# ScalarE's order of work in two edge convolutions, and node ranks from a product with a step matrix instead of 49 gathers

## The reference, cut to what matters

```python
def mesh_conv(x, src, dst, ea, w1, b1, g, bt, w2, b2):
    m = jnp.concatenate([x[dst], x[src], ea], axis=-1) @ w1 + b1
    m = jax.nn.silu(group_norm(m, g, bt))          # 8 groups of 16
    m = m @ w2 + b2
    out = jax.ops.segment_sum(m, dst, num_segments=n)
    cnt = jax.ops.segment_sum(jnp.ones((dst.shape[0],), m.dtype), dst, num_segments=n)
    return out / jnp.clip(cnt, 1.0)[:, None]
h = mesh_conv(x, ...); h = silu(group_norm(h)) + time embedding
h = mesh_conv(h, ...); h = silu(group_norm(h)) + x          # then attention, then GAT
```

## Time and profile before

| | us |
|---|---|
| median of three runs | 11735.4 |
| the runs | 11731.89 to 11742.31 |
| profiled execution, its own time | 11847.93 |
| its span in the trace | 11846.2 |
| `prepare` and `n_first`, span's start to the first gather of convolution 1 | 238.64 |
| convolution 1, first gather to the last copy of sums | 238.64 to some 2730 |
| last copy of sums of convolution 2 | 5343.66 |

### The profile page before, as it was taken

The page is one execution under the profiler, slowest core; times in us unless marked ns, Lnnn a source line. Parts: engine busy times, 40 slices in busy tenths (PEclk is TensorE's granted clock), DMA queues, the critical chain, the costliest instruction groups (busy, mean ns, idle before and its releaser), DMA issues. The chain is left out here.

```text
span 11846.2 us, 181243 instructions
## 1 busy us (share of the span) xinstructions
PE 8134.7 (69%) x44314; PEld 6471.6 (55%) x44314; DVE 6838.3 (58%) x16254; ACT 4174.9 (35%) x19386; POOL 6469.9 (55%) x6618
## 2 busy tenths in 40 slices
PE   2677777775777777774666666666467777777775
PEld 1455455553555555553555555555367667777774
DVE  4677777775777777775545555555633333333336
ACT  0344444442444444441222222222123333333332
POOL 4666666662666666642555555554155555555551
PEclk7888888887888888886777777777578788888886
DMA  4344344442434444433554444554344444444443
GB/s 109 107 113 114 112 112 114 113 114 60 113 112 114 113 113 113 113 97 107 144 146 144 143 143 143 144 144 115 84 94 96 96 95 98 97 96 98 99 97 89
DMA packets 1667963, 1323.24 MB, mean 112 GB/s; under 512 B 578730, under 2 KB 1444339, under 8 KB 1666782
## 3 DMA queue, kind: packets, MB, share of 16 engines
q1 hardware_dynamic: 1427212, 770.46, 23.7%
q0 software_dynamic: 237088, 539.87, 17.6%
q10 hardware_dynamic: 2610, 1.32, 0.1%
HBM read 1250.67 MB, written 60.09 MB: 111 GB/s over the span
## 5 line engine op out<-in xcount | busy, mean ns | idle before, releaser
L537 POOL DMA_INDIRECT conv_gath<-b,plan x3232 | 3060.8, 947 | 2007.9 <-issue 866.6
L890 POOL DMA_INDIRECT gat_gath<-g,idx x1616 | 1756.4, 1087 | 1540.6 <-DVE gat_val L1171 861.2
L890 POOL DMA_INDIRECT attn_gath<-kv,plan x1616 | 1528.5, 946 | 1429.6 <-DVE attn_val L1171 746.3
L573 PE MATMUL conv_sums<-conv_hot,conv_m 128*128 128x128 f32 x6464 | 1271.8, 359 | 1261.0 <-ACT acc L610 553.5
L573 PEld LDWEIGHTS conv_sums<-conv_hot,conv_m 128*128 128x128 f32 x6464 | 1100.2, 257 | 1670.5 <-issue 1670.4
L593 ACT ACTIVATE conv_sq<-conv_z 128x512 f32<-128x512 f32 x808 | 482.2, 597 | 2276.7 <-PE conv_z L563 1917.9
L925 PE MATMUL gat_p_edge<-weta,plan 128*128 128x136 f32 x3232 | 862.8, 355 | 522.0 <-ACT gat_edge L1000 255.8
L656 DVE TENSOR_REDUCE conv_var<-conv_sq 128x32 f32<-128x512 f32 x808 | 549.4, 680 | 1153.2 <-ACT conv_sq L593 960.5
L560 PEld LDWEIGHTS conv_z<-conv_win,conv_hotT 128*128 128x128 f32 x6464 | 923.1, 205 | 514.0 <-issue 514.0
L1025 ACT COPY small<-attn_smalls 40x127 f32 x1616 | 417.3, 258 | 1987.8 <-remote 1490.4
L556 PE MATMUL conv_z<-conv_wblock,conv_ea 128*128 128x512 f32 x1616 | 988.1, 698 | 82.6 <-DVE conv_hotT L647 37.9
(11 more groups left out here) (370 smaller groups left out, 15956.4 us busy)
## 6 DMA issues: line engine op xcount, KB each, us to landing
conv_win<-a SPq DMA_DIRECT2D x3232, 64.0 KB
conv_places<-places SPq DMA_DIRECT2D x202, 512.0 KB
attn_win<-q SPq DMA_DIRECT2D x1616, 64.0 KB
plan<-in_xeT SPq DMA_DIRECT2D x404, 256.0 KB
conv_gath<-b,plan POOLq DMA_INDIRECT x3232
attn_places<-places SPq DMA_DIRECT2D x101, 512.0 KB
plan<-places SPq DMA_DIRECT2D x404, 128.0 KB
attn_gath<-kv,plan POOLq DMA_INDIRECT x1616
```

Source lines behind the costliest of these rows:

```text
L537: pool.indirect_dma_start(gath[:, b.c * BQ + k, t, :], None, b_table, bass.IndirectOffsetOnAxis(ap=C["src"][:, b.quad(k) * QT + t:b.quad(k ...
L573: mm = nc.tensor.matmul(sums[g % SQ][:, t * P:(t + 1) * P], m[:, g % BQ, t * P:(t + 1) * P], hot[:, g % BQ, t, :], start=True, stop=True)
L890: pool.indirect_dma_start(gath[:, b.c * BQ + k, t, :], None, table, bass.IndirectOffsetOnAxis(ap=rows, axis=0))\
```

## The change

In `conv_edges`, ACT's order becomes, for each p: square of 2p+4, copies of quads 2p-2 and 2p-1, SiLU of 2p, square of 2p+5, SiLU of 2p+1, with one turn of the loop fewer. No instruction is added or taken away there, and PE's, DVE's and POOL's orders stay.

The tile in which a node falls is now found in `prepare` without gathers. Two small DMAs bring the 1616 first-node numbers as 101 rows of 16, and the same rows moved by one. POOL writes the node numbers 0 to 6271 in 101 partitions. DVE forms the differences of the rows (`steps`, 101x17) and a 101x6272 matrix that is 1 where a batch begins below a node (`reached`). 49 matmuls of 101x128 by 101x17 add up the steps, which gives for each node the 16 first-node numbers of its batch and the number of the batch. DVE finds the tile from that (ten operations). The destinations' 49 gathers stay in `n_first` and no longer wait for anything there; part 0 of the count stands behind group 4 instead of 5.

```diff
 # prepare, SyncE
             sp.wait_ge(padded, 1)
+            by_batch = w["n0_b"].rearrange("o (k t) -> (o k) t", t=TB)
+            sp.dma_start(starts_k[:, 0, :], by_batch).then_inc(starts_loaded, 16)
+            sp.dma_start(starts_k[1:NBATCH, 1, :], by_batch[0:NBATCH - 1, :]).then_inc(starts_loaded, 16)
+            sp.wait_ge(padded, 2)
             for dst, src in edge_loads:
 # prepare, GpSimd
             pool.iota(node_i[:, :], pattern=[[P, NBLK]], base=0, channel_multiplier=1).then_inc(pool_made, 1)
+            pool.iota(nodes_i[:, :], pattern=[[1, NP]], base=0, channel_multiplier=0).then_inc(nodes_made, 1)
 # prepare, TensorE
+            pe.wait_ge(reached_made, 1)
+            for part, (b0, b1) in enumerate(RANKED):
+                for b in range(b0, b1):
+                    mm = nc.tensor.matmul(p_n[part][:, (b - b0) * (TB + 1):(b - b0 + 1) * (TB + 1)],
+                                          reached[:, b * P:(b + 1) * P], steps[:, :], start=True, stop=True)
+                mm.then_inc(starts_ready, 1)
             pe.wait_ge(loaded, LOADS)
 # prepare, VectorE
+            nc.vector.memset(starts_k[0:1, 1, :], 0).then_inc(padded, 1)
             nc.vector.memset(dst_q[:, :], N).then_inc(padded, 1)
...
+            dve.wait_ge(starts_loaded, 2 * 16)
+            link(nc.vector.tensor_copy(first_k[:, :], starts_k[:, 0, 0:1]))
+            link(nc.vector.memset(first_k[0:1, :], -1.0))
+            link(nc.vector.tensor_tensor(steps[:, 0:TB], starts_k[:, 0, :], starts_k[:, 1, :], ALU.subtract))
+            link(nc.vector.memset(steps[:, TB:TB + 1], 1.0))
+            dve.wait_ge(nodes_made, 1)
+            link(nc.vector.tensor_scalar(reached[:, :], nodes_i[:, :], first_k[:, 0:1], None, ALU.is_gt))
+            dve.sem_inc(reached_made, 1)
             dve.wait_ge(edges_loaded, EDGE_LOADS)
-            link(nc.vector.tensor_copy(n0_f[:, :], n0_all[:, :].rearrange("p (k t) -> p k t", t=TB)[:, :, 0]))
-            link(nc.vector.tensor_tensor(below[:, :, 0:NBATCH], bc(n0_f[:, :].unsqueeze(1), wide),
-                                         bc(node[:, :].unsqueeze(2), wide), ALU.is_lt))
-            link(nc.vector.tensor_reduce(batch[:, :], below[:, :, 0:NBATCH], AX.X, ALU.add))
-            link(nc.vector.tensor_scalar(batch[:, :], batch[:, :], -1.0, 0.0, ALU.add, ALU.max))
-            link(nc.vector.tensor_copy(batch_i[:, :], batch[:, :]))
...
             dve.sem_inc(places_made, 1)
+            for part, (b0, b1) in enumerate(RANKED):
+                dve.wait_ge(starts_ready, part + 1)
+                link(nc.vector.tensor_tensor(below[:, bs, 0:TB], pn[:, :, 0:TB], bc(node[:, bs].unsqueeze(2), wide), ALU.is_lt))
+                link(nc.vector.tensor_reduce(tile[:, 0, bs], below[:, bs, 0:TB], AX.X, ALU.add))
+                # ... and three more small operations to tile_i
 # conv_edges, ScalarE
-            for p in range(-2, NPAIR + 2):
-                g = 2 * p - 4
+            for p in range(-2, NPAIR + 1):
+                g = 2 * p - 2
...
+                square(2 * p + 4)
                 copies(g, starts)
                 copies(g + 1, starts)
                 silu(2 * p)
-                square(2 * p + 4)
+                square(2 * p + 5)
                 silu(2 * p + 1)
-                square(2 * p + 5)
 # n_first, GpSimd
                 for part, (b0, b1) in enumerate(RANKED):
-                    for b in range(b0, b1):
-                        pool.indirect_dma_start(n0_rows[:, b, :], ...)
-                for part, (b0, b1) in enumerate(RANKED):
-                    pool.wait_ge(tile_found, part + 1)
                     for b in range(b0, b1):
                         pool.indirect_dma_start(dst_rows[:, b, :], ...)
 # n_first, VectorE
-                    if g == 1:
-                        find_tiles(dve, link, 0)
-                    if g == 3:
-                        find_tiles(dve, link, 1)
-                    if g == 5:
+                    if g == 4:
                         rank(dve, link, 0)
```

More of the change, by code:

```diff
@@ L203, in prepare @@
         node_i = st.sb("node_i", [P, NBLK], I32)
-        n0_f = st.sb("n0_f", [P, NBATCH])
-        node, below, batch, batch_i = (R[n] for n in ("node", "below", "batch", "batch_i"))
+        starts_k = st.sb("starts_k", [NBATCH, 2, TB], I32)
+        first_k = st.sb("first_k", [NBATCH, 1])
+        steps = st.sb("steps", [NBATCH, TB + 1])
+        nodes_i = st.sb("nodes_i", [NBATCH, NP], I32)
+        reached = st.sb("reached", [NBATCH, NP])
+        node, below, tile_i = (R[n] for n in ("node", "below", "tile_i"))
         tile, shift, corner = (R[n] for n in ("tile", "shift", "corner"))
@@ L226, in prepare @@
         p_rep = st.ps("p_rep", [P, 512])
+        p_n = [st.ps(f"p_n{n}", [P, 512]) for n in range(2)]
+        starts_loaded, nodes_made, reached_made, starts_ready = (
+            st.sem(n) for n in ("starts_loaded", "nodes_made", "reached_made", "starts_ready"))
         edges_loaded, loaded, stored = st.sem("edges_loaded"), st.sem("loaded"), st.sem("stored")
@@ L366, in _ @@
             link = Chain(dve, chain)
-            wide = [P, NBLK, NBATCH]
+            nc.vector.memset(starts_k[0:1, 1, :], 0).then_inc(padded, 1)
             nc.vector.memset(dst_q[:, :], N).then_inc(padded, 1)
@@ L395, in _ @@
             dve.sem_inc(places_made, 1)
+            for part, (b0, b1) in enumerate(RANKED):
+                bs, wide = slice(b0, b1), [P, b1 - b0, TB]
+                dve.wait_ge(starts_ready, part + 1)
+                pn = p_n[part][:, 0:(b1 - b0) * (TB + 1)].rearrange("p (b t) -> p b t", t=TB + 1)
+                link(nc.vector.tensor_tensor(below[:, bs, 0:TB], pn[:, :, 0:TB], bc(node[:, bs].unsqueeze(2), wide), ALU.is_lt))
+                link(nc.vector.tensor_reduce(tile[:, 0, bs], below[:, bs, 0:TB], AX.X, ALU.add))
+                link(nc.vector.scalar_tensor_tensor(tile[:, 0, bs], pn[:, :, TB], float(TB), tile[:, 0, bs], ALU.mult, ALU.add))
+                link(nc.vector.tensor_scalar(tile[:, 0, bs], tile[:, 0, bs], -1.0 - TB, 0.0, ALU.add, ALU.max))
+                link(nc.vector.tensor_copy(tile_i[:, bs], tile[:, 0, bs]))
             link(nc.vector.memset(mask[:, :, :], -BIG))
@@ L1377, in node_stage @@
         if kind == "first":
-            n0_gathered, dst_gathered = ([st.sem(f"{n}{h}") for h in range(2)] for n in ("n0_gathered", "dst_gathered"))
-            tile_found, ranked, degree_ready, rank_chain = (
-                st.sem(n) for n in ("tile_found", "ranked", "degree_ready", "rank_chain"))
+            dst_gathered = [st.sem(f"dst_gathered{h}") for h in range(2)]
+            ranked, degree_ready, rank_chain = (st.sem(n) for n in ("ranked", "degree_ready", "rank_chain"))
         LOADS = 16 * {"first": 1, "conv1": 0, "conv2": 1, "attn": 3, "gat": 3}[kind]
@@ L1748, in node_stage @@
         if kind == "first":
[L1749 to L1762, removed]
+            node, below, tile = (R[n] for n in ("node", "below", "tile"))
+            dst_rows, tile_i, degree = (R[n] for n in ("dst_rows", "tile_i", "degree"))
             def rank(dve, link, part):
@@ L1783, in _ @@
                 for part, (b0, b1) in enumerate(RANKED):
-                    for b in range(b0, b1):
-                        pool.indirect_dma_start(n0_rows[:, b, :], None, w["n0_b"].rearrange("o (k t) -> (o k) t", t=TB),
-                                                bass.IndirectOffsetOnAxis(ap=batch_i[:, b:b + 1], axis=0))\
-                            .then_inc(n0_gathered[part], 16)
-                for part, (b0, b1) in enumerate(RANKED):
-                    pool.wait_ge(tile_found, part + 1)
                     for b in range(b0, b1):
@@ L1858, in build @@
             R = {"node": kept("node", [P, NBLK]), "below": kept("below", [P, NBLK, P]),
-                 "n0_rows": kept("n0_rows", [P, NBLK, TB], I32), "dst_rows": kept("dst_rows", [P, NBLK, P], I32),
-                 "batch": kept("batch", [P, NBLK]), "batch_i": kept("batch_i", [P, NBLK], I32),
+                 "dst_rows": kept("dst_rows", [P, NBLK, P], I32),
                  "tile": kept("tile", [P, 2, NBLK + 1]), "tile_i": kept("tile_i", [P, NBLK], I32),
```

## The result

The changed kernel takes 11,641.3 us (median of 4 runs, 11,636.3 to 11,657.3) against 11,738.0 us before (median of 4). The ratio is 0.992, with a 95% interval of 0.9903 to 0.9938, so the gain is some 97 us, or 0.8%. The forecast was 11,670 us, a gain of 64, in a range of 11,560 to 11,790. Sign and range held. The two terms of the sum were off in opposite directions, and one step of the reasoning behind them was wrong: about half of the gain came from a part that the sum had at 8 us.

What follows compares the result with a forecast made beforehand. POOL's gathers were taken to bound the steady convolutions. `prepare` -7.4, `n_first` -48.4, tails -8 and steady pairs 0 made -64 us, so 11735.4 became 11,670 us, in a range of 11,560 to 11,790.

Steps and rivals of the forecast that it cites:

- The gathers set the steady cycle: Steady convolutions: a gather costs 1.4 to 1.5 us, and eight of them are the cycle of a pair.
- The low rival: Convolutions: ACT's order holds the cycle, which would fall to 10.0 us a pair, 10,910 us in all; chance 0.06.
- So I take zero for the steady pair: Steady convolutions: the new ACT order gains nothing per pair; at most 0.2 us a pair, -76 us.
- Reading two: Steady convolution 1: cycles with slower and faster PE sums last 11.91 and 11.96 us, so PE's loop isn't the bound.
- the rival on a late PE: Convolutions: sums start behind a SiLU, z misses the release, 12.4 us a cycle, 11,840 us in all; chance 0.14.
- The loop that remains is shorter: Convolutions: the loop through ACT and PE takes about 5.2 us instead of 8.7 after the change.
- Tails: End of each convolution: two quads of copies fewer behind ACT's last SiLU, 4.2 us, twice, -8 us.
- `prepare`: Tile search in `prepare`: -11.4 + 3.7 + 0.3 = -7.4 us, between -3 and -8.
- the cover that the text called tight: `prepare`: the 49 matmuls must end before DVE reaches the tile search near 28 us; otherwise some 4 us come back.
- the prediction's own last line: Wrong if steady cycles change by more than 0.2 us, or the 49 matmuls hold DVE before its tile search.
- `n_first`: First node stage: first gather to convolution 1 takes 129 us instead of 177.4, -48.4 us.
- the gathers were hidden anyway: `n_first`: its groups 2 to 6 take the time, gathers only lie beside them; -15 us, 11,720 us; chance 0.10.

Runs made afterwards that it cites:

- first profile: The unchanged kernel before, as profiled ahead of the prediction: 11,847.9 us.
- second profile: The kernel before, unchanged, profiled once more: 11,733.1 us.
- ranks alone: Kernel before with only the new node ranks, ScalarE's order as before: 11,692.3 us, ratio 0.9962.
- order alone: Kernel before with only ScalarE's new order in the convolutions, ranks as before: 11,677.6 us against 11,738.8, ratio 0.9954.

## Why the prediction was right, and where it wasn't

- **The gathers set the steady cycle:** shown. Three, four and five gathers give 1956, 2408 and (new order) 2947 us. The low rival, 10,910 us by ScalarE's order, is out: even where the order helps, the cycle stops at 11.8 us.
- **"So I take zero for the steady pair":** this step failed. The old order lost 0.22 us in every second cycle to a late z. I had its price among the bounds (0.1 to 0.2 us a pair), but as a faster rate of the gathers, and it is a wait. It came to 35 us in the two convolutions, where the sum had 0.
- **Reading two,** that the cycle is indifferent to PE's half speed, held in the profile that it was read from and not in the next. In the first profile 6 of 175 cycles have z within 0.3 us of the next gather, and yet the others take 11.98 us; in the second, cycles with z in time take 11.82 and those with a late z 12.06, in turn. In the first execution POOL's idle time behind the eight gathers is 2.29 us in cycles with z in time, against 2.12 in the second, and that much more slack z had. Two neighbouring cycles of one profile, 11.91 and 11.96 us, couldn't show it. The same holds of "against: these cycles cost nothing now" in the rival on a late PE: in the second profile they did cost, and the change relieved them instead of making them worse. What the change gives in an execution like the first is not shown.
- **The loop that remains is shorter:** as argued. The last z of a cycle ends over 1.2 us ahead of the next gather in 171 of the changed kernel's 177 steady cycles of convolution 1, and never within 0.3 us; the added 16 matmuls a pair made none late. The tail without gathers takes 9.2 us a pair, 9.03 before.
- **Tails:** -4.2 us each forecast, -5.3 and -6.8 measured.
- **`prepare`:** -7.4 forecast, -4.6 measured in the first profile's terms. The missing part is the cover that the text called tight, 3.34 us of waiting for the 49 matmuls; with the search moved, 2.3 us of them came back. By the prediction's own last line, which names the 49 matmuls holding DVE before its tile search as a sign of being wrong, this part was wrong. The comparison was priced at 6.7 and took 3.54 us, hidden either way.
- **`n_first`:** 129 us forecast, 182.58 - 56.66 = 125.9 measured. The term was right against the profile used, but that one had the longest stage of seven; against the average the ranks gave 49 us. That the gathers were hidden anyway is out. (The parts listed for the time behind the first 69.5 us add up to 58.8, not 59.5.)
- **The sum:** -56 and -8 forecast; ranks alone -47 (-28 to -61 by its interval, 0.24% to 0.52% of 11,739 us), order alone -61 (-39 to -70, 0.33% to 0.60%). The errors of the terms partly cancelled: the ranks gave 9 us less than forecast and the order 53 more. That the forecast came within 30 us of the measurement owes something to luck, and the reason given for nothing in the steady cycles didn't hold.

What stays open: why more matmuls on PE, with no z late, lengthen a cycle bound by gathers (11.74, 11.81 and 11.95 us with 4, 16 and 32 window matmuls a pair). And why some 15% of the changed kernel's cycles take 12.03 instead of 11.81 us, with z early in them too.

## What to carry to other kernels

Where a cycle is held by one resource, another chain that ends close to its release may hold part of the cycles: look at many cycles, and sort their lengths by how late that chain was, before calling it free. A distance to the release that is the same in every such cycle is the sign that the chain holds it. Take a second profile of the kernel before where a term rests on one stage's length. Of two edits that each remove the same wait, try each alone: together they may make a loop that neither had.

## What the runs showed of the hardware

A gather of 128 rows that the profile shows as 0.94 us, issued every 1.25 us, cost 1.38 us more a cycle for each gather between eight and ten, 1.40 in the rank stage and 1.48 in the 64 at a convolution's start. The difference appears as idle time of POOL and of whoever waits, after the burst (2.1 us behind eight, 2.4 behind ten, 10.25 behind 64). TensorE's granted clock rose from 0.86 to 0.94 in the old order and from 0.87 to 0.97 in the new when 16 matmuls a pair were added, and fell from 0.86 to 0.79 when 12 were taken away. So work added to an engine that was busy for 1615 of 2160 us came in part for nothing.
